# Fused attention and fp8 layer on one core: a new order of SP's loads, a divided last PV, and three steps moved on VectorE and ScalarE

## The reference

```python
xn = _layernorm(x, axis=-1)
qkv = xn @ w_qkv.T + b_qkv                     # 16 heads of 16
att = q @ k.T / sqrt(16) + hope_bias           # bias per head, depends on i - j
att = softmax(where(causal, att, -inf))
attn = (att @ v).reshape(B, T, C) @ w_proj.T + b_proj
x_q, k_q = (xn.bf16 / s_in).fp8_e4m3, (kernel / s_k).fp8_e4m3
ffn = (x_q @ k_q * (s_in * s_k)).bf16 + bias
out = x + attn + ffn
```

## Time and profile before

| | |
|---|---|
| median of 3 runs | 825.46 us (824.64 to 831.89) |
| profiled execution | 820.26 us, span of its instructions 818.5 us |
| PE busy | 747.2 us, 91% |
| DVE busy | 628.9 us, 77% |
| ACT busy | 581.0 us, 71% |
| POOL busy | 528.2 us, 65% |
| DMA | 106.07 MB, 130 GB/s over the span |
| granted TensorE clock, mean | 0.973 |

### The profile page before, as it was taken

How to read it: one execution, slowest core, us unless ns; L and a number is a source line. 1 busy time by engine, 2 the same in 40 slices (tenths; PEclk the granted TensorE clock), 3 DMA queues, 4 the chain that set the end, 5 groups by cost and what they waited for, 6 DMA issues and landing times.

```text
span 818.5 us, 23154 instructions
## 1 busy us (share of the span) xinstructions
PE 747.2 (91%) x6313; PEld 510.0 (62%) x6313; DVE 628.9 (77%) x2395; ACT 581.0 (71%) x1258; POOL 528.2 (65%) x525
## 2 busy tenths in 40 slices
PE   6869999999999999999999999999999999999883
PEld 3546666666676667657676666657666666767552
DVE  3767878887977878788788878787787879778722
ACT  4236767777786877778687777778677777867671
POOL 6433568567666867667676757766685776667580
PEclk8859999999999999999999999999999999999998
DMA  6834666567566656666566657756665775666502
GB/s 170 165 68 95 114 145 123 129 148 144 127 138 153 118 130 138 138 145 137 141 121 151 123 127 162 142 126 137 148 117 123 155 143 124 139 130 121 120 24 86
DMA packets 55548, 106.07 MB, mean 130 GB/s; under 512 B 10464, under 2 KB 30432, under 8 KB 55520
## 3 DMA queue, kind: packets, MB, share of 16 engines
q1 hardware_dynamic: 53192, 102.96, 60.4%
q10 hardware_dynamic: 2328, 2.77, 1.0%
HBM read 18.68 MB, written 8.91 MB: 34 GB/s over the span
## 4 chain that ended last, share of the span: by engine, by line
PE 49%; ACT 15%; SPq 11%; issue 9%; DMA 7%; DVE 5%; ACTq 3%; DVEq 1%; POOL 0%; POOLq 0%
SPq L328 11%; PE misc_a L539 8%; PE misc_a L655 8%; PE scoreT_b L629 6%; PE misc_b L539 6%; ACT probs L911 6%; PE scoreT_a L629 3%; DMA stacks<-neg_max_T 3%; PE misc_b L655 3%; PE score_a L606 3%; PE score_c L606 2%; ACT qk_parts L818 2%; ACT out_T L884 2%; ACT attn_hi L893 2%; ACT xnT_hi L807 1%
## 5 line engine op out<-in xcount | busy, mean ns | idle before, releaser
L1187 POOL TENSOR_SCALAR_AFFINE_SELECT probs<-probs 128x512 f32<-128x512 f32 x256 | 159.5, 635 | 244.7 <-ACT probs L911 242.8
L989 DVE CUSTOM_DVE_ANT_0 score_b<-score_b,causal_mask_q 128x384 f32<-128x384 f32 (+3 forms) x321 | 161.9, 521 | 119.6 <-PE score_b L606 118.4
L989 DVE CUSTOM_DVE_ANT_0 score_a<-score_a,causal_mask_q 128x512 f32<-128x512 f32 x319 | 173.1, 559 | 8.1 <-PE score_a L606 4.1
L911 ACT ACTIVATE probs<-scoreT_b 128x384 f32<-128x384 f32 (+1 forms) x256 | 134.5, 525 | 60.7 <-issue 23.7
L989 DVE CUSTOM_DVE_ANT_0 score_c<-score_c,causal_mask_q 128x256 f32<-128x256 f32 (+3 forms) x384 | 171.4, 474 | 2.3 <-PE score_c L606 2.2
L911 ACT ACTIVATE probs<-scoreT_a 128x512 f32<-128x512 f32 (+1 forms) x256 | 145.6, 569 | 14.0 <-PE scoreT_a L632 7.4
L989 DVE DVE_READ_ACCUMULATOR2_ANT row_max<- 128x1 f32 x1024 | 142.9, 140 | 0.0
L911 ACT ACTIVATE probs<-scoreT_c 128x384 f32<-128x384 f32 (+1 forms) x256 | 136.2, 532 | 3.7 <-PE scoreT_c L632 3.3
L655 PE MATMUL misc_a<-probs,v_ones 128*32 128x128 f32 (+3 forms) x1536 | 131.2, 438 | 0.4 <-POOL probs L1187 0.4
L629 PE MATMUL scoreT_a<-stacks 64*128 64x512 f32 (+3 forms) x320 | 108.3, 358 | 21.8 <-DMA stacks<-neg_max_T 13.8
L629 PE MATMUL scoreT_b<-stacks 64*128 64x384 f32 (+3 forms) x320 | 119.5, 393 | 7.6 <-ACT probs L911 7.1
(11 more groups left out here) (241 smaller groups left out, 1948.9 us busy)
## 6 DMA issues: line engine op xcount, KB each, us to landing
stacks<-qk_parts SPq DMA_DIRECT2D x128, 512.0 KB, 8.1
x_ring<-in_L_attn_x SPq DMA_DIRECT2D x16, 512.0 KB, 3.6
xn<-recips SPq DMA_DIRECT2D x31, 256.0 KB
out<-x_ring SPq DMA_DIRECT2D x15, 512.0 KB, 3.0
attn<-out_T SPq DMA_DIRECT2D x48, 128.0 KB, 2.6
stacks<-neg_max_T SPq DMA_DIRECT2D x128, 4.0 KB
attn<-out_T ACTq DMA_DIRECT2D x16, 128.0 KB, 2.9
low_features<-neg_max_T SPq DMA_DIRECT2D x124, 4.0 KB
```

The source lines that it names most:

```text
L911: A(probs_slot(g, k), STB[(SLOTS * g + k) % 3][:, 0:w], ACT.Exp).then_inc(exp_done, 1)
L989: last = V.tensor_tensor_reduce(bank, bank, CMQ[:, T - w:T], 1.0, LEAST, ALU.add, ALU.max, MX[:, g % 2, 8 * h + 4 + qt:8 * h + 5 + qt])
L1187: last = GP.affine_select(out=d, in_=d, compare_op=ALU.is_ge, fill=0.0, base=0, pattern=[[0, HU], [1, P]], channel_multiplier=-1)
```

## The change

Four tables and the order of SP's body change.

- `PV_AT[3]` goes from (0, 3) to (0, 0), and `PV_REST_AT` gets unit 3: its tile 0 is done in slot (0, 0) of the next batch, its tiles 1 to 3 in slot (0, 3), with the transposition of unit 1's maxima between. The order of the jobs, and so their banks, stays as it is.
- `XL_AT`: T_lo(0) comes behind the chunk of slot (3, 9) and not of (3, 10); T_lo(1) behind that of (3, 11) and not of (0, 0) of the next batch.
- `MAX_AT` becomes a list: in unit 0 of a batch ACT copies the maxima (those of unit 1) ahead of the exp of slot 1 and not of slot 2.
- On SP, `load_x(b + 2)` with its two waits stands ahead of `store_recips(b - 1)`, and `spread_recips(b - 1)` stands behind `load_stack(b + 1, 0)`.

```diff
@@ -49,9 +49,9 @@
 
 
 
-PV_AT = [(1, 0), (2, 3), (3, 3), (0, 3)]
-
-PV_REST_AT = {0: (1, 3)}
+PV_AT = [(1, 0), (2, 3), (3, 3), (0, 0)]
+
+PV_REST_AT = {0: (1, 3), 3: (0, 3)}
 MT_AT, FIRST_MT_AT = [(0, 3), (1, 3), (2, 3), (3, 3)], (0, 5)
 QK_AT = [(0, 6), (0, 9), (1, 6), (1, 9)]
 V_AT = [(2, 6), (2, 9)]
@@ -63,7 +63,7 @@
 OUT_AT = 4
 FIRST_MT_OUT_AT = (0, 6)
 
-MAX_AT, FIRST_MAX_AT = 2, (0, 4)
+MAX_AT, FIRST_MAX_AT = [1, 2, 2, 2], (0, 4)
 QK_HI_AT, QK_LO_AT = [(0, 6), (0, 9), (1, 6), (1, 9)], [(0, 7), (0, 10), (1, 7), (1, 10)]
 V_OUT_AT = [(2, 6), (2, 9)]
 AH_AT = [(2, 2), (2, 3)]
@@ -71,7 +71,7 @@
 RESULT_AT = [(3, 1), (3, 6)]
 NORM_AT = [(3, 1), (3, 3), (3, 4), (3, 6)]
 XH_AT, FIRST_XH_AT = [(3, 9), (3, 10)], [(0, 2), (0, 2)]
-XL_AT, FIRST_XL_AT = [(3, 10), (0, 0)], [(0, 3), (0, 3)]
+XL_AT, FIRST_XL_AT = [(3, 9), (3, 11)], [(0, 3), (0, 3)]
 
 INVERT_AT, LAST_INVERT_AT = (0, 8), (3, 8)
 STATS_AT, AGGR_AT = [(1, 2), (1, 3), (1, 5), (1, 8)], (1, 9)
@@ -462,20 +462,20 @@
                     sp.wait_ge(st_ready, ROW * b)
                 load_stack(b, 3)
                 load_max(b, 1)
-                if not first:
-                    store_recips(b - 1)
                 if load:
                     if not first:
                         sp.wait_ge(out_stored, 16 * b)
                     sp.wait_ge(x_loaded, 16 * (b + 2))
                     load_x(b + 2)
                 if not first:
-                    spread_recips(b - 1, last)
+                    store_recips(b - 1)
 
                 if not last:
                     wait_alone(sp, (w_loaded, 16), (st_ready, ROW * b + SLOTS),
                                (ql_ready, 4 * (b + 1) + 2))
                     load_stack(b + 1, 0)
+                if not first:
+                    spread_recips(b - 1, last)
                 load_max(b, 2)
                 regroup(b, 0, first)
 
@@ -896,7 +896,7 @@
                 for g in range(G):
                     for k in range(SLOTS):
                         pb, pg = (b, g - 1) if g else (b - 1, 3)
-                        if (g, k) == FIRST_MAX_AT if first and g == 0 else k == MAX_AT:
+                        if (g, k) == FIRST_MAX_AT if first and g == 0 else k == MAX_AT[g]:
                             if not (last and g == 3):
                                 max_hi(*((b, g + 1) if g < 3 else (b + 1, 0)))
                         if k == OUT_AT and not (first and g == 0):
```

## The result

The changed kernel takes 876.84 us (median of 4 runs, 875.13 to 880.46) where the kernel before takes 827.25: a ratio of 1.060, with a 95% interval of 1.054 to 1.066. I had forecast 818.5, with 810 to 828 for 8 cases in 10 and 0.08 for slower by over 1%. From one x issue to the next a batch of the hardware loop took 47.1 us on average and now takes 51.0. In what follows a time is the median of all runs of a kernel, and a ratio, to runs of the kernel before made beside it, leaves the few slow runs out, so the two need not agree to the last digit.

The account below looks back on a forecast made before the run. PE, busy 91% of the span, was taken to bound the kernel. SP's new order (4.8 us) and the last unit's divided PV (2.2) gave 7.0 us off 825.46: 818.5 us, with 810 to 828 for 8 in 10.

Parts of the forecast that it names:

- What bounds the kernel: Whole run: PE, busy 91% of the span, bounds it; only what shortens PE's own sequence shortens the run.
- x sooner on SP: SP's queue: x issued 4.8 us sooner, at no cost to PE; with the spread's move, 4.8 us off the run.
- the sum: Whole run: 4.8 us from SP's order plus 2.2 us from the last unit's PV make 7.0 us.
- The first 0.6 us of the wait are free: PE's wait for the maxima, slot (2, 0): only the part beyond 0.60 us costs, 0.32 us a batch.
- The spread behind the stacks: SP's queue: two spread issues take at most 1.86 us, maxima's DMAs start by 400.95; SP loses 0.3 us or nothing.
- The spread's landing: Inverses' spread behind the stacks: lands about 407.9, 408.4 at worst; POOL's divide ends at 410.3, counted at nothing.
- rival D: Spread lands after 408.0, holding POOL's divide, DVE's quantiser step, then PE: 8 us slower, 833; chance 0.12.
- cannot pass: DMA queue: descriptors are consumed in ring order, so the spread cannot pass the stacks; no size given.
- The divided PV: Slots (0, 0) to (0, 3): tile 0 covers PE's 0.62 us wait, DVE becomes releaser; gain 0.15 a batch, 2.2 us.

Follow-up runs that it names:

- e6: The changed kernel with the spread one step further back, behind the maxima of unit 2: 907.5 us, ratio 1.099.
- e12: e8 with the spread issued one slot later on ScalarE's queue, ahead of slot (1, 2) and not (1, 1): 900.4 us, ratio 1.094.
- e2: The kernel before with one edit, load_x ahead of store_recips: 819.5 us, ratio 0.994.
- e4: The changed kernel with the spread put back ahead of load_stack(b + 1, 0), x sooner and the tables kept: 821.0 us, ratio 0.996.
- e5: The changed kernel with each spread cut to 8 of its 512 columns, 1/64 of the bytes: 835.5 us, ratio 1.012.
- e9: The changed kernel with each spread cut to 8 rows of 2 KB, where it had 128 rows: 829.3 us, ratio 1.008.
- e7: The changed kernel with 10 further matmuls on PE ahead of its wait for the maxima of unit 2: 857.1 us, ratio 1.038.
- e10: The changed kernel with the maxima of unit 2 issued by GpSimd on its own queue, the spread still behind the stacks on SP: 865.7 us, ratio 1.055.
- e8: The changed kernel with the spread issued by ScalarE on its own queue, ahead of its exp of slot (1, 1): 820.6 us, ratio 0.996.
- e3: The kernel before with the change's tables alone (divided PV, T_lo sooner, unit 1's maxima copied sooner), SP's order as before: 824.7 us, ratio 0.999.

## Why the prediction was wrong

**What bounds the kernel**: right. PE's wait at slot (2, 0) decided in the changed kernel and in most of the others. In e6 it was the wait for POOL's masks and in e12 that for ScalarE's copy, each made by the experiment.

**x sooner on SP**: right in direction and size. x went out where I had it, DVE's waits for it went from 10 to 1, and e2 gives 4.8 us, the 4.8 of the sum; with an interval of 1.9 to 7.8 the equal digits are luck. The reason was only half right. I had the maxima's issues at 3.5 to 5.5 us because a quarter of the bytes ahead was gone. In e2 and e4, which have that quarter less and the spread ahead of the stacks, they still take 6.4 and 6.3 on average, against 6.9 before. That half microsecond is what fell; from the last issue to PE's start it stays at 1.1 us or more.

**"The first 0.6 us of the wait are free"**: not contradicted, also beyond the case it came from. By it the cost over the 0.6 is 0 for x sooner (7.8 us of waits in all), 15 x (24.5/15 - 0.6) = 15.5 us for e5, 8.1 for e9 (17.1 us of waits). Measured from e4, by the ratios times 825 us, they are 13 and 10, each with some 6 to either side. For e7, where the clock is full, the changed kernel's 42.8 us of waits give 34, and 35 was measured, with 7 to either side. The intervals are too wide to tell 0.6 from 0.4 or 0.8.

**The spread behind the stacks**: the step that failed. I wrote "the two spreads at most 1.86 (...), so the maxima's DMAs start at 400.95 at the latest (...): SP loses 0.3 us or nothing". The spread's two issues took 6.46 us there, and the maxima's DMAs started 8.0 us behind the first stack and not 3.1 (400.95 - 397.85). I took an issue's length from the place it stood in and carried it to another. The row that spoke against it was in my own group: four maxima take 6.78 us behind the stacks and 3.35 elsewhere. I put that down to the bytes ahead, though an issue that is held holds whatever is behind it. Had I read the 6.78 as a property of the place, the moved spread would have inherited it: two issues until some 8 us after the stacks, and the maxima's first issue 6.5 us later than before. Since the maxima are not held behind that, their last issue is only 2.4 us later; the spread's bytes add the rest of PE's longer wait.

**The spread's landing**: also short. I had 1.3 us for its 0.5 MB and a landing 10 us after the first stack's issue; the divide starts 429.92 - 417.41 = 12.5 us after it. The Trainium skill's sentence on ring order ("DMA: Bandwidth & Descriptors", Queues, rings and completion order), which I had set beside rival D, fits what is seen on SP's queue; it says nothing of a held issue, and it adds that a later descriptor may finish its write before an earlier one, so my "cannot pass" said more than the page. The same page (Issuing engines are not separate DMA queues) says that issuing from several engines saves only the sequencer's time. e10 agrees: issued 3.6 us sooner on GpSimd's queue, the 16 KB let PE go on only 0.5 us sooner. e12 differs from it, and there the measurement decides: not even the sequencer's time was saved, 4.29 us against the 1.24 of e8.

**The clock**: missing in the sum and in every rival. PE had stood idle for up to 1.6 us a batch at full clock; I did not ask what 2.7 us would do. It took the clock to 0.5 for 3.4 or 6.8 us of each batch (I wrote "after each" 6.8 in what I expected of e7; five of the 14 were 3.4). e7 prices it at some 18 of the 53 us.

**The rivals**: D was the right place, with 0.12 and a price of 8 us over. Its mechanism (the late divide) is real, e6 shows it at ratio 1.10; in the changed kernel the divide and the maxima are late together, and PE's wait shows the maxima. From e4 to the changed kernel it is 0.064 by the ratios, some 53 us: 13 for the held issue alone (e5), 35 - 13 = 22 for the spread's bytes ahead of the maxima and the divide, 53 - 35 = 18 for the clock. Each share has 6 to 8 us to either side. How the 22 are divided between the late maxima and the late divide is not shown, since e10 did not part them.

**The divided PV**: the mechanism was right where it was placed, and its gain was lost again. The 2.2 us of the sum are not seen. Slots (0, 3), (0, 4) and (0, 7) of the changed kernel:

```profile
406.54 0.50 PE L606 MATMUL score_a<-stacks 64*128 64x512 f32 x1 [0.22 <-DVE row_max L989]
...
408.82 0.44 PE L629 MATMUL scoreT_b<-stacks 64*128 64x384 f32 x1
...
411.91 0.44 PE L629 MATMUL scoreT_b<-stacks 64*128 64x384 f32 x1 [0.35 <-ACT probs L911]
```

The 0.62 us of the earlier trace rows are gone, VectorE releases slot (0, 3) in ACT's place as I wrote, and slot (0, 3) to (0, 4) takes 2.28 us where it took 3.14, tile 0 having gone ahead of it. From slot (0, 0) to (0, 4) that leaves 408.82 - 403.27 = 5.55 us, where it was 5.67 before. Then PE waits 0.35 us for an exp in slot (0, 7), which it did not before, and slot (0, 4) to (0, 7) takes 3.09 us where it took 2.88: what was gained is given back three slots on. e3 finds 0.7 us for all the tables together, the maxima's copy in slot (0, 1) included, with an interval of 3 us to either side.

## What to carry to other kernels

Moving a DMA in a queue moves its issue into another neighbourhood, and the length of the issue belongs to the neighbourhood: read what any issue takes there, and give that to the newcomer and to all behind it. Ask of a wait that grows not only what it costs, but whether PE's idle stretch takes the clock with it. And when an experiment changes the queue, compare the time of issue too: e8 and e12 differ by one slot, 0.3 us ahead of the first stack or 1.1 behind it, and by 80 us.

## What the runs showed of the hardware

- Behind two 512 KB copies from SBUF to SBUF, further DMA issues of SP and of ScalarE are held for microseconds, whatever their size: two issues of SP take 6.25 us at 4 KB each (e5), 5.75 at 16 KB each in 8 rows (e9) and 6.46 at 256 KB each (the changed kernel), where 1.31 is what they take 8 us behind the copies (e6). Such issues are all through 5.4 us (e12) to 9.3 us (the slowest batch of the kernel before) after the first copy's issue. ScalarE, held so, runs no activation (3.98 us idle in e12).
- GpSimd's issues in the same stretch are not held (2.24 us for four in e10), but each 4 KB issued so landed 3.9 to 5.6 us after its issue while the stacks and the spread were moving.
- PE idled 2.71 us, and the granted clock was 0.5 for 6.8 us from within that stretch on, with PE busy in most of it (the changed kernel). With idle stretches of 1.6 to 1.8 us a batch it stayed at 1.00 from 176 to 776 us (e5). With ten matmuls of no use in the longer gap it stayed at 1.00 too, and the kernel was some 18 us faster for 160 matmuls more (e7).
